# Output projection of an attention block by seven block products per pair of heads instead of eight

## What is computed

```python
x = x + _L0_xattn_ref(_layernorm(x), ctx, Wq, Wk, Wv, Wo)   # 16 batches, 256 rows, D 512, 16 heads of 128
x = x + _L0_ffn_ref(_layernorm(x), w_gate, w_up, w_down)    # block-scaled (MX) quantised, inner width 2048

ctx = jnp.einsum('bhqk,bkhd->bqhd', attn, v).reshape(b, sq, H * HD)
return ctx @ Wo                                             # the output projection: 256 x 2048 by 2048 x 512
```

## Time and profile before

| | |
|---|---|
| median of three runs | 2036.09 us |
| profiled execution | 2035.61 us, span 2034.0 us |
| PE busy | 2016.0 us (99%), 15422 matmuls |
| DVE / ACT / POOL busy | 1528.0 (75%) / 1001.8 (49%) / 739.9 us (36%) |
| granted TensorE clock | 1.00 throughout |
| start of head 32, 64, 128 and 240 on PE | 219.5, 430.6, 849.1 and 1583.3 us |
| first FFN matmul on PE | 1693.3 us |

### The profile page before, as it was taken

How to read it: one execution, slowest core, us unless ns; L and a number is a source line. 1 busy time by engine, 2 the same in 40 slices (tenths; PEclk the granted TensorE clock), 3 DMA queues, 4 the chain that set the end, 5 groups by cost and what they waited for, 6 DMA issues and landing times.

```text
span 2034.0 us, 44904 instructions
## 1 busy us (share of the span) xinstructions
PE 2016.0 (99%) x15422; PEld 1508.8 (74%) x15422; DVE 1528.0 (75%) x3341; ACT 1001.8 (49%) x2679; POOL 739.9 (36%) x877
## 2 busy tenths in 40 slices
PE   8999999999999999999999999999999999999999
PEld 6888878788888887878888888888888885444444
DVE  6767777777777777777777777776656557899886
ACT  8955554554555545545554555545555443333332
POOL 5413333332333233333333333322111104878776
PEclk9999999999999999999999999999999999999999
DMA  8834344444444444444444354534233354555555
GB/s 253 219 63 92 83 97 87 84 92 91 88 89 91 92 91 86 87 89 91 87 81 102 73 105 77 104 71 94 53 84 58 68 133 98 91 87 94 93 91 99
DMA packets 456111, 193.74 MB, mean 95 GB/s; under 512 B 419456, under 2 KB 432256, under 8 KB 455904
## 3 DMA queue, kind: packets, MB, share of 16 engines
q1 hardware_dynamic: 433984, 140.31, 36.3%
q0 software_dynamic: 15584, 44.45, 8.8%
q10 hardware_dynamic: 6336, 6.29, 1.0%
HBM read 61.21 MB, written 27.26 MB: 43 GB/s over the span
## 4 chain that ended last, share of the span: by engine, by line
PE 93%; DVE 2%; DMA 2%; ACT 1%; issue 1%; POOL 0%; DVEq 0%; ACTq 0%; SPq 0%; POOLq 0%
PE b_qk L1085 33%; PE b_v L1085 17%; PE b_c L1085 10%; PE b_s L1085 9%; PE b_o L1140 8%; PE b_w L1140 8%; PE b_o L1211 3%; PE b_w L1211 2%; PE b_pt L1085 2%; PE b_x L1085 2%; DMA probT<-psplit 1%; ACT psplit L663 0%; DVE nmax L917 0%; ACT prob L653 0%; DVE kvT L755 0%
## 5 line engine op out<-in xcount | busy, mean ns | idle before, releaser
L1085 PE MATMUL b_qk<-kvT,attn_weights 128*128 128x256 f16 x3072 | 377.2, 273 | 3.7 <-DVE qk L755 2.9
L1085 PE MATMUL b_v<-attn_weights,kvT 128*128 128x256 f16 x3072 | 377.2, 273 | 0.0
L1085 PE MATMUL b_qk<-xT,attn_weights 128*128 128x256 f16 x3072 | 377.2, 273 | 0.0
L653 ACT ACTIVATE prob<-b_s,nmax 128x256 f32<-128x256 f32 x514 | 239.3, 470 | 278.2 <-DVE nmax L917 276.3
L1085 PEld LDWEIGHTS b_qk<-kvT,attn_weights 128*128 128x128 f16 x3072 | 300.2, 98 | 92.9 <-issue 5.1
L944 DVE SCALAR_TENSOR_TENSOR psplit<-prob,rrec,psplit 128x256 f16<-128x256 f32 x514 | 306.0, 636 | 79.6 <-ACT psplit L663 79.6
L755 DVE SCALAR_TENSOR_TENSOR qk<-b_qk,qk 128x512 f16<-128x512 f32 x256 | 176.7, 690 | 246.0 <-ACT qk L609 236.0
L609 ACT ACTIVATE qk<-b_qk 128x512 f16<-128x512 f32 x256 | 152.6, 596 | 423.4 <-PE b_qk L1085 423.0
L1085 PEld LDWEIGHTS b_qk<-xT,attn_weights 128*128 128x128 f16 x3072 | 300.6, 98 | 34.8
L1085 PEld LDWEIGHTS b_v<-attn_weights,kvT 128*128 128x128 f16 x3072 | 300.6, 98 | 34.8
L663 ACT ACTIVATE psplit<-prob,rrec 128x256 f16<-128x256 f32 x514 | 233.3, 501 | 69.2 <-DVE rrec L937 69.2
(11 more groups left out here) (131 smaller groups left out, 2685.8 us busy)
## 6 DMA issues: line engine op xcount, KB each, us to landing
ffn_w<-wffn SPq DMA_DIRECT2D x48, 256.0 KB, 2.8
acc<-xtok POOLq DMA_DIRECT2D x16, 512.0 KB, 4.7
out<-acc POOLq DMA_DIRECT2D x16, 512.0 KB, 3.3
xrow<-xtok POOLq DMA_DIRECT2D x31, 256.0 KB, 3.1
kvrow<-kvt POOLq DMA_DIRECT2D x61, 128.0 KB, 2.4
out<-attn_weights POOLq DMA_DIRECT2D x28, 256.0 KB, 5.4
stage<-wattn SPq DMA_DIRECT2D x12, 512.0 KB, 4.4
ffn_scratch<-ffn_t SPq DMA_DIRECT2D x48, 128.0 KB, 2.4
```

The costliest lines, as they stand in the source:

```text
L653: last = eng.activation(half(prob, q, 256), half(bS, q, 256), ACT.Exp, bias=nmax[:, q:q + 1], scale=1.0, accum_out=rsum[:, q:q + 1])
L1085: last = eng.matmul(out, l, r, start=(a == 0), stop=(a == len(pairs) - 1))
```

## The change

From batch 2 on, the output projection of a pair of heads is no longer one product of 256 rows x 256 inputs by 256 x 512, but seven products of 128 x 128 blocks by 128 x 256 blocks, whose sums and differences give the same result (Strassen's and Winograd's kind of scheme). The parts:

- **PE.** `project` for such a pair runs in two calls, one head later than before: `project_fast(u, 0)` with four products and `project_fast(u, 1)` with three, each product three matmuls of 256 columns: 21 matmuls of 256 columns in place of 12 of 512. The first two batches (pairs 0 to 15) are as before. The products accumulate over eight pairs in b_pt, b_x, b_o and b_w. The wait of the context for `c_lo` becomes one for `c_hi`.
- **Left operands.** ACT writes the context rows in f32 (`evict_rows`, into `blocks`) in place of f16; `cbuf`'s low part on DVE goes. Per pair POOL makes five block sums in three instructions (`left_sums`: 256, 256 and 128 columns), ACT the high parts of seven blocks in one (`left_hi`, 896 columns), DVE the low parts in one (`left_lo`, 896 columns), both at even k after the probabilities' parts.
- **Right operands.** In quads 4 to 7 the eight weight pieces are loaded again, summed (POOL `out_sums`), split (ACT `out_hi`, `out_sums_hi`; DVE `out_lo`, four instructions) and stored to a scratch in HBM. They no longer fit in SBUF whole: two of the eight pairs' blocks stay resident, six are reloaded in every batch into two slots (`load_slot`, 512 and 384 KB per pair, on SP after that head's `transpose_p`).
- **Batch's end.** Two adds of 512 columns become twelve of 256 (`add_products`), all in the boundary quad: four ahead of and four behind the rest of head k = 1, four in head k = 2. There `ffn_y` moves to k = 2 and `ffn_magic` to k = 3. POOL stores the rows in q = 1. For the last batch one add stands behind each of the FFN's first twelve pairs.
- **DVE's loop** now covers the batches s = 3 to 12.
- **FFN.** Its weight tiles go through quads 8 to 55 instead of 4 to 51. Gate and up rotate over two pairs of banks up to u = 27, over three from then on, since the products hold b_pt, b_x, b_o and b_w. `NO_DOWN` becomes 0 to 3, 44, 47, 50, 53, 56, 59 (ten left over). The last rows' steps come ten pairs later.

The core of the diff:

```diff
-FFN_FROM, FFN_TO = QPB, QPB + FFN_TILES
+FFN_FROM, FFN_TO = 2 * QPB, 2 * QPB + FFN_TILES
-NO_DOWN = (0, 1, 2, 3, 36, 40, 44, 48)
+NO_DOWN = (0, 1, 2, 3, 44, 47, 50, 53, 56, 59)
-GU_BUF = [u % 2 if u < 4 else (u - 2) % 3 for u in range(2 * PAIRS)]
+GU_BUF = [u % 2 if u < THIRD else (u - THIRD + 2) % 3 for u in range(2 * PAIRS)]
+TERMS = (("m1", "a0+b1", 3), ("m3", "a0", 2), ("m4", "b1", 1), ("m2", "a1+b1", 0)), \
+    (("m5", "a0+b0", 4), ("m7", "b0-b1", 6), ("m6", "a0-a1", 5))
 # tensor
+            def project_fast(u, part):
+                batch, first_, last_ = u // 8, u % 8 == 0, u % 8 == 7
+                slot, use = slot_use(u)
+                eng.wait_ge(sm[f"slot_loaded{slot}{part}"], 16 * use)
+                if part == 0:
+                    eng.wait_ge(sm["s_lo"], u - FAST_PAIR + 1)
...
+                if first_ and batch > FAST:
+                    eng.wait_ge(sm["m_added"], 3 * (batch - 1 - FAST) + (2, 3)[part])
+                for name, rows, block_ in TERMS[part]:
+                    at = LEFT[rows] * P
+                    for z, (a, b) in enumerate(PARTS):
+                        last = eng.matmul(product_at[name], left_part(u % 2, a)[:, at:at + P], slot_w(slot, block_, b),
...
 # vector
+            def left_lo(n, k):
+                eng.wait_ge(sm["s_hi"], 2 * n + k // 2 - 1 - FAST_PAIR)
+                eng.tensor_tensor(left_part(k // 2, 1).rearrange("p (n f) -> p n f", f=P), blocks[:, 1:8, :],
+                                  left_part(k // 2, 0).rearrange("p (n f) -> p n f", f=P), ALU.subtract
+                                  ).then_inc(sm["s_lo"], 1)
+            def add_product(b, name, sign, tile_, side, behind):
+                if behind is not None:
+                    eng.wait_ge(sm["m_step"], 12 * (b - FAST) + behind)
+                a = acc[:, bass.ds(((b + 1) & 1) * (2 * D) + tile_ * D + side * 256, 256)]
+                eng.scalar_tensor_tensor(out=a, in0=product_at[name], scalar=sign * O_OUT, in1=a, op0=ALU.mult,
+                                         op1=ALU.add).then_inc(sm["m_step"], 1)
 # in quad(n), q == 1: add_products group 0 ahead of kv_lo and group 1 behind p_lo at k == 1, group 2 at k == 2
+                    if sums and k in (1, 2):
+                        add_products(s - 1, 2 * k - 2)
-                    if ffn and k == 2:
+                    if ffn and k == 2 + sums:
                         ffn_magic(w)
-                    if ffn and k == 1:
+                    if ffn and k == 1 + sums:
                         ffn_y(w)
+                    if (front or k < 3) and k % 2 == 0 and fast(n, k, 4):
+                        left_lo(n, k)
+                    if sums and k == 1:
+                        add_products(s - 1, 1)
 # scalar
+            def evict_rows(n, k):
+                eng.wait_ge(sm["c_done"], i + 1)
+                if k % 2 and not (isinstance(n, int) and i == FAST_HEAD + 3):
+                    eng.wait_ge(sm["s_lo"], 2 * n + (k - 3) // 2 - FAST_PAIR)
...
 # gpsimd
+            def left_sums(n, k):
+                wait_apart(eng, "c_hi", 4 * n + k + 1)
...
+                eng.tensor_tensor(blocks[:, 4:6, :], blocks[:, 1:9:7, :], blocks[:, 0:4:2, :], ALU.add)
+                eng.tensor_tensor(blocks[:, 6:8, :], blocks[:, 0:2, :], blocks[:, 2:9:6, :], ALU.subtract)
+                eng.tensor_tensor(blocks[:, 3, :], blocks[:, 1, :], blocks[:, 2, :], ALU.add)
```

429 lines of the change are left out of this document (305 added, 124 removed).

## The result

The changed kernel takes 2045.1 us (median; 2042.5 to 2047.1) against 2035.7 us (2034.7 to 2036.6) of the kernel before, measured beside it: 1.0046 times, 95% interval 1.0034 to 1.0059. It is 9.4 us slower. The forecast was 2028 us, faster, and the range ended at 2044. The profiled executions have spans of 2044.5 and 2034.0 us.

A forecast was written before the change was run, and what follows sets the result against it. PE's own instructions were taken as the bound. Against the profiled 2035.61 us: -33.4 + 17 + 1 + 5 + 1 + 2 = -7.4, forecast 2028 us; the range for 8 in 10 was 2008 to 2044 us.

The forecast's parts named there:

- PE, -33.4: Output projection on PE: 0.30 us less per pair of heads, for 112 pairs, so 33.4 us saved.
- The boundary quad, +17: DVE at the batch's end: PE waits 1.7 us a batch, 17 us (3 to 35) over ten looped batches.
- The walk: Step-by-step timing of DVE through the boundary quad's heads, giving PE waits of 1.7 us a batch.
- with POOL in the way once more in two heads: Upper case for the boundary quad: 1.7 + 2 x 0.9 = 3.5 us a batch.
- only four times in the whole run: Sign given for the rival of 2010 us (chance 0.23): how often PE waited for DVE before the change.
- Head 3 and the next quad just hold: Boundary quad's end: they start 5.5 us in and just hold, with remnants of 0.2 to 0.4 us.
- Written-out boundary quads, +1: Three boundary quads outside DVE's loop, with register wait 0.15 instead of 0.8: 0.3 each, 1 us.
- Right operands, +1 (0 to 4): Quads 4 to 7 do these instead of FFN tiles; DVE has 2 us more a quad, costing 1 us.
- Junction, +5 (1 to 8): Passage to the FFN: with two bank pairs PE waits for DVE; 5.8 less 0.84 already there, 5 us.
- the walk's 2.1 and 1.1: Junction to the FFN: PE waits of 2.1 and 1.1 us expected at u = 6 and 8.
- Reloads, +2: Weight blocks reloaded on SP for six of eight pairs: 2 us (0 to 6) added for transposition waits.
- the boundary quad tips over: Rival, chance 0.19: POOL slides against psplit and left_lo, ACT hands over late; 4 us a batch, 2051 us.

The follow-up runs named there:

- e15: Changed kernel, loop kept, POOL's block sums earlier, x1 scale factors behind the next quad's sums, weight load ahead of store: 2027.2 us, 0.9963 of before.
- e13: Changed kernel, DVE's loop written out, POOL's block sums earlier, x1 scale factors behind next quad's sums, weight load ahead of store: 2018.5 us, 0.9918 of before.
- e7: Changed kernel, DVE's loop written out, out_hi later, POOL's block sums earlier, x_rescale a quad later, last batch's adds spread over pairs 3 to 12: 2034.5 us.
- e9: Changed kernel with SP's load of the next weight piece ahead of the 896 KB store of split blocks: 2042.95 us, 1.0038 of before.
- e5: Changed kernel with ACT's out_hi in quads 4 to 7 moved behind the high part of the probabilities: 2047.4 us, 1.0062 of before.
- e10: Changed kernel with ffn_magic of the boundary quad moved behind the last head's vector work: 2087.1 us, 1.0259 of before.

## Why the prediction was wrong, step by step

- **PE, -33.4: right.** Call times 1.31 and 0.99 us, heads 6.55 and 6.22, quads 25.54 against 26.14: 0.60 a quad.
- **The boundary quad, +17: the step that failed.** It lost 31.2 us in ten batches, 3.1 each. The walk had 1.7, and 3.5 as its other end "with POOL in the way once more in two heads". That end was the nearer one, and the trace of before had a row for it:

```profile
POOL ffn_b L471 <- DMA ffn_t<-ffn_b: 181.8, 47, 5.4
```

POOL stood there at the FFN tile's last operation in 47 of 48 tiles, until a DMA had moved the tile before. The walk put POOL's sums where their input is ready, and not where POOL's queue lets them start. e15 shows what the order is worth: in another order the same instructions lose 16.5 us, and e13, with the loop written out, 7.8. That 16.5 is also the 17 of the walk is in part luck: 0.6 us a batch of it stand in the quad behind, where the walk had nothing.
- **A deadline left out.** The walk asked only when PE wants the low part of q and k and the first product. PE also wants the low part of v for `context`, and 14.5 of its 29 us of waiting for DVE stand there. The rows showed no sign to go by: before the change it was one wait of 0.3 us. That PE waited for DVE "only four times in the whole run" counts the waits for the low part of q and k alone.
- **"Head 3 and the next quad just hold": wrong**, +1.25 us in the quad behind (part of the 3.1 above). The rescale of the row sums was taken at 0.17 us everywhere; moving `ffn_magic` in front of it put POOL's rounding beside it, and it takes 1.08. The x1 scale factors, ahead of the block sums on POOL, are the other part there (e13 against e7). The diff moved a step by one head, and I followed its own duration but not what it releases.
- **Written-out boundary quads, +1: too low.** Batch 13, the one with an FFN tile, lost 2.3 us; batches 14 and 15, without one, nothing.
- **Right operands, +1 (0 to 4): wrong, 5.1** (130.7 to 135.8 us). I had priced DVE's two us and not that GpSimd stands for the load of each piece, 14 us at most. e9 shows that the store issued ahead of it is 2.2 of this; e5 that ACT's order isn't. The rest stays open.
- **Junction, +5 (1 to 8): mechanism right, size within the bounds, 7.2** (349.4 to 356.6; 353.8 and 354.9 in other runs of nearly the same code). The two stalls for `b_qk` at 1714 and 1720 us are the walk's 2.1 and 1.1, as 1.85 and 2.02. The 1.7 us of the lower clock behind them were not in the walk; without them it is 5.5.
- **Reloads, +2: too high, about 0.** PE's waits for transpositions fell from 3.1 to 0.7 us, and where DVE was no longer late (e13, e15) they were 3.9 and 3.6.
- What the sum lacked on the other side: the stalls of before (1049.4 - 1045.6 = 3.8 us in the ten batches, 0.7 ahead of them) go away with it. -33.4 + 31.2 + 3 (written-out batches, 277.6 where 43 undisturbed heads take 274.6) + 5.1 + 7.2 - 4.5 = +8.6, against 9.4 measured.

The rival "the boundary quad tips over" had the mechanism (POOL slides against `psplit`, ACT and DVE hand q and k over late) at 4 us a batch, and said that it decides from 2.5 us on. It was at 3.1. I gave it 0.19, because three ordinary quads were to return the time. The third and fourth nearly did (25.75 and 25.62 us, with a floor of 25.54); the quad directly behind did not.

## What to carry to other kernels

When work is moved onto an engine near its limit, walk every queue it depends on from that queue's own last stop, not from the moment when the input is ready: here the same instructions cost +9 us in one order and -8 us in another. Prices of four disturbances in one stretch don't add: taking one of three away returned 59 to 72% of the loss, the fourth 31%, so leaving out one of them doesn't name the cause. The run that names it does all the work in another order (e15). And where a step is moved, look at what its result releases and who runs beside that. A stall can cost twice: in e10 nine of ten stalls of 3.4 us were followed by at least 3.4 us at the lower clock, which cost some 1.7 us more.
